# Two transposes moved behind a half product, and finer warming matmuls, in a conditional mix followed by a 6-bit linear layer

## The chip, the core and the metric

The kernel runs on one core of a Trainium2 chip. The metric is the time of one execution on the device in microseconds (us), the median of several runs. The engines are named as in the profile: PE is the matrix engine, PEld its weight loads, DVE the vector engine, ACT the scalar engine, POOL the GpSimd engine, SP the engine that issues most of the DMAs. An instruction that loads the stationary operand of a matmul is called a weight load here, whatever the operand holds.

## What is computed

The input x has 64 samples of 64 channels by 1024 columns. Each sample picks one of 16 matrices (64 by 64) and mixes its channels with it. The result goes through a linear layer whose 1024 by 1024 weights are 6-bit integers, packed four to three words of int32, with a scale and a zero point for each output column; x is added at the end:

```python
W = weights[condition]                                  # (64, 64, 64)
y = einsum('bct,bcd->bdt', x, W)
w = (unpacked.astype(float32) - zero_point) * scale     # 6 bits per weight
out = x + einsum('bsk,nk->bsn', y, w) + bias
```

All inputs and outputs are float32.

## The kernel before, in words

Two samples are one tile of 128 rows, so there are 32 tiles, in groups of four (`RING = 4`). The first group is written out by hand; a loop `Fori(1, TRIPS)` runs over the seven others. Every engine has its own program, the order of the instructions in it is the order in the text, and engines wait for each other by semaphores alone; no planner reorders anything.

For a tile PE does a `mix` (matmuls of 64 by 64, which give the mixed tile with k on the partitions, in PSUM). ACT takes its upper part (`high`, `y_hi`), DVE the rest (`low`, `y_lo`), and `products` multiplies both with the integer weights `qT`, for the left 512 or the right 512 output columns: 8 values of kt times the two parts, so 16 matmuls of 512 columns for one half of one tile. DVE scales the result (`scale_out`) and adds x, bias and the term of the zero points (`add_residual`); SP stores it.

The weights are prepared in the first group only. DVE unpacks a block of 128 output columns (`unpack_q(n)`, n from 0 to 7), PE transposes it by eight matmuls against an identity (`transpose_q(n)`, L269 to L276, into one of two PSUM banks in turn), and ACT turns it into floats and puts it into `qT` (`place_q(n)`, L440). The left half of the outputs needs blocks 0 to 3, the right half 4 to 7. `transpose_q(n)` waits for the three parts of `unpack_q(n)` and for `place_q(n - 2)`, which empties its bank. `sum_x(j)` (L411) is an ACT pass that sums the rows of tile j's input for the term of the zero points; PE's `sum_y` waits for all four of them.

Ahead of all this PE multiplies a block of zeros (`keep_warm`, L346) nine times while the first block of weights is loaded and unpacked, and twice more behind `transpose_q(0)`. Around the change PE's program reads (L375 to L395): blocks 4 and 5; the first half of tile 1's left product; block 6; the second half; block 7; the mixes of tiles 2 and 3; the sums; then the first right half, which needs all eight blocks. ACT's program reads there (L461 to L467): place blocks 4 and 5, sum tile 2, place block 6, sum tile 3, place block 7, `high` of tile 2.

Of the kernel before, what the change touches and what calls it, by code (L numbers as in the profile page):

```python
# [22 lines left out]
I16 = mybir.dt.int16  # L23

P = 128
WARMUP = 9
QCENTER = 32.0
QMASK = 63
QBITS = 6
# [3 lines left out]
def adaln_ffn(nc: bass.Bass, x, cond, weights, qweight, scale, zero, bias, out):  # L33
    B, C, K = x.shape
    NCOND, _, S = weights.shape
    N, KP = qweight.shape
    assert C == S == P // 2 and N == K
    G = KP // 3
    KT = K // P
# [11 lines left out]
    with ExitStack() as ctx:  # L51
        def sb(name, shape, dt):
            return ctx.enter_context(nc.sbuf_tensor(name, shape, dt))
# [4 lines left out]
        def sem(name):  # L58
            return ctx.enter_context(nc.semaphore(name))
# [16 lines left out]
        warm = sb("warm", [P, 512], BF16)  # L76
# [7 lines left out]
        def y_bank(slot, half):  # L84
            return y_ps[:, slot, half, :, :].rearrange("p t r -> p (t r)")
# [5 lines left out]
        free_banks = [y_bank(2, half) for half in range(2)]  # L91
# [43 lines left out]
        o_ps_ready = [sem(f"o_ps_ready{h}") for h in range(H)]  # L135
# [6 lines left out]
        def x_arrived(eng, j, i):  # L142

            eng.wait_ge(x_loaded[j % RING], (i + j // RING + 1) * 16)


        def load_q(eng, n):
            eng.dma_start(q_raw[:, n, :], qweight[n * P:(n + 1) * P, :]).then_inc(q_loaded[n], 16)
# [4 lines left out]
        def load_w_half(eng, slot, half, entry):  # L153
            rows = slice(half * S, (half + 1) * S)
            eng.dma_start(w_sb[rows, slot, :],
                          weights[bass.ds(entry, 1), :, :].rearrange("a c s -> (a c) s")
                          ).then_inc(w_loaded[slot], 16)

        def pick(eng, at):
            return eng.value_load(ids[0:1, bass.ds(at, 1)], min_val=0, max_val=NCOND - 1)  # L160

        @block.sync
        def _(sp):
# [27 lines left out]
            def store_last():  # L191
                t = TILES - 1
                store(t % RING, t // RING, 0)
                for n, (_, col, width) in enumerate(last_pieces):
                    sp.wait_ge(o_ready[1], t + 1 + n)
                    sp.dma_start(out_rows[t * P:(t + 1) * P, col:col + width],
                                 o_sb[:, t % RING, col:col + width]).then_inc(o_stored[1][t % RING], 16)
# [45 lines left out]
        def _(pe):  # L243
            def wait_mix(j, i):

                t = i * RING + j
                x_arrived(pe, j, i)
                pe.wait_ge(w_loaded[j % RING], (i + j // RING + 1) * 32)
                if not isinstance(t, int) or t >= 2:
                    pe.wait_ge(y_lo_ready, (t - 1) * 2)  # L250
# [18 lines left out]
            def transpose_q(n):  # L269
                pe.wait_ge(q_part, 3 * (n + 1))  # L270
                if n >= 2:
                    pe.wait_ge(qt_ready, n - 1)
                for kt in range(KT):
                    last = nc.tensor.transpose(qt_banks[n % 2][:, kt, :], q_cols[:, n % 4, kt * P:(kt + 1) * P],  # L274
                                               ident[:])
                last.then_inc(qt_ps_ready, 1)  # L276
# [12 lines left out]
            def products(bank, col, width, slot, kts=range(KT), parts=(y_hi, y_lo)):  # L289
                for kt in kts:  # L290
                    for part in parts:
                        last = nc.tensor.matmul(bank, part[:, slot, kt, :], qT[:, kt, col:col + width],  # L292
                                                start=(kt == 0 and part is y_hi),
                                                stop=(kt == KT - 1 and part is y_lo))
                return last
# [47 lines left out]
                last.then_inc(o_ps_ready[1], 1)  # L343


            def keep_warm(times):  # L346
                for _ in range(times):
                    nc.tensor.matmul(free_banks[1], warm[:, 0:P], warm[:], start=True, stop=True)

            def left_half(kts):  # L350
                return products(o_ps[:, 0, :], 0, NH, 1, kts)
# [2 lines left out]
                return products(o_ps[:, 0, 0:2 * P], 0, 2 * P, 0, parts=(part,))  # L354

            pe.wait_ge(warm_ready, 1)
            keep_warm(WARMUP)
            pe.wait_ge(ident_ready, 1)
            transpose_q(0)
            keep_warm(2)  # L360
            wait_mix(0, 0)
            mix(0, y_banks[0])
            transpose_q(1)
# [12 lines left out]
            transpose_q(5)  # L376
            pe.wait_ge(left_copied, 1)
            pe.wait_ge(y_lo_ready, 4)
            left_half(range(0, KT // 2))
            transpose_q(6)  # L380
            left_half(range(KT // 2, KT)).then_inc(o_ps_ready[0], 1)
            transpose_q(7)
            for j in (2, 3):
                wait_mix(j, 0)
# [24 lines left out]
        @block.scalar  # L409
        def _(act):  # L410
            def sum_x(j, i):  # L411
                x_arrived(act, j, i)
                if not isinstance(i, int) or i * RING + j >= RING:
                    act.wait_ge(ysum_ps_ready, (i * RING + j - RING + 1) * 2)
                if not isinstance(i, int) or i * RING + j >= 2:
                    act.wait_ge(xsum_ready, i * RING + j - 1)
                nc.scalar.activation(junk[:, j % 2, :], x_sb[:, j % RING, :], ACT.Copy,  # L417
                                     accum_out=xsum[:, j % RING:j % RING + 1]).then_inc(xsum_ready, 1)

            def high(j, i, banks, halves=range(2)):  # L420
                t = i * RING + j
                for half in halves:

                    act.wait_ge(y_ps_ready, t * 2 + half + 1)
                    cols = slice(half * S, (half + 1) * S)
                    nc.scalar.activation(y_hi[:, j % RING, :, cols], banks[half],  # L426
                                         ACT.Copy).then_inc(y_hi_ready, 1)

            def copy_sums(half, banks, i):

                rows = slice(half * C, (half + 1) * C)
                act.wait_ge(ysum_ps_ready, (i + 1) * 2 * RING)
                for odd in range(2):
                    place = (half + odd) % 2
                    last = nc.scalar.activation(ysum[rows, odd:RING:2],
                                                banks[half][place * S:(place + 1) * S, odd:RING:2],
                                                ACT.Copy, scale=-1.0)
                last.then_inc(ysum_ready[half], 1)

            def place_q(n):  # L440
                act.wait_ge(qt_ps_ready, n + 1)
                nc.scalar.activation(qT[:, :, n * P:(n + 1) * P], qt_banks[n % 2].bitcast(I16), ACT.Copy,  # L442
                                     bias=-QCENTER).then_inc(qt_ready, 1)

            for n in range(2):
                load_q(act, n)
            act.wait_ge(warm_ready, 1)
            nc.scalar.activation(junk[:, 1, 0:1], warm[:, 0:1], ACT.Copy)
            act.wait_ge(ids_loaded, 16)
            load_w_half(act, 0, 1, pick(act, 1))  # L450
            for n in (2, 3, 5, 7):
                load_q(act, n)
            place_q(0)
            high(0, 0, y_banks[0], range(1))
            place_q(1)
            place_q(2)
            sum_x(0, 0)
            place_q(3)
            high(1, 0, y_banks[1])
            sum_x(1, 0)  # L460
            place_q(4)  # L461
            place_q(5)
            sum_x(2, 0)
            place_q(6)
            sum_x(3, 0)
            place_q(7)
            high(2, 0, y_banks[0])  # L467
            for half in range(2):
                copy_sums(half, free_banks, 0)
            high(3, 0, y_banks[1])  # L470
            for j in range(RING):
                sum_x(j + RING, 0)

            def step(i, sums=True):
                for j in range(RING - 1):
                    high(j, i, y_banks[j])
                act.wait_ge(resid_ready, i * RING)
                for half in range(2):
                    copy_sums(half, sum_banks, i)
                high(RING - 1, i, y_banks[RING - 1])  # L480
                if sums:
                    for j in range(RING):
                        sum_x(j + RING, i)

            with act.Fori(1, TRIPS - 1) as i:
                step(i)
            step(TRIPS - 1, sums=False)
# [187 lines left out]
```

## Time and profile before

| | us |
|---|---|
| median of 3 runs | 286.48 |
| lowest, highest | 285.56, 287.77 |
| the profiled execution, whole | 285.53 |
| its span, from the first to the last instruction | 283.7 |
| PE busy | 276.5 (97% of the span) |
| DVE busy | 191.6 (68%) |
| POOL busy | 99.1 (35%) |
| ACT busy | 83.8 (30%) |

The page's clock is 1.00 in every slice. The first group takes about 40 us of the span, the loop the rest. The difference of 1.8 us between the profiled execution and its span lies around the first and the last instruction. Times within the trace are counted from the first instruction.

### The profile page before, as it was taken

How to read it: one execution, taken by the hardware profiler on the slowest of the kernel's cores; microseconds unless marked ns; L12 is line 12 of the kernel's file. 1: busy time of each engine (PE TensorE's matmuls, PEld its weight loads, DVE VectorE, ACT ScalarE, POOL GpSimd, SP SyncE). 2: the span in 40 equal slices, each digit the busy share in tenths (PEclk: the TensorE clock that was granted, in tenths of full speed). 3: DMA queues.
4: the chain of work that ended last, by engine and by line, in shares of the span. 5: the costliest groups of instructions: out<-in, count | busy, mean ns of one | idle time of the engine just before them, and what ended most of it. 6: DMA issues, size and time to landing. Idle time of an engine off the chain costs nothing.

```text
span 283.7 us, 8499 instructions
## 1 busy us (share of the span) xinstructions
PE 276.5 (97%) x3307; PEld 231.1 (81%) x3307; DVE 191.6 (68%) x261; ACT 83.8 (30%) x169; POOL 99.1 (35%) x41
## 2 busy tenths in 40 slices
PE   6999999999999999999999999999999999999995
PEld 2888887788888887988888888888888888888885
DVE  2898897785566556865559555676667655595554
ACT  3795334232044300633017310443106330060000
POOL 4005903964430444314442444404443044430000
PEclk9999999999999999999999999999999999999999
DMA  7930563456115541355114551144413552101112
GB/s 274 375 120 13 178 230 124 152 158 232 75 74 157 163 178 70 114 158 194 74 74 124 165 210 74 74 155 157 157 68 109 165 203 96 74 37 74 74 74 75
DMA packets 20278, 37.96 MB, mean 134 GB/s; under 512 B 6814, under 2 KB 7070, under 8 KB 20266
## 3 DMA queue, kind: packets, MB, share of 16 engines
q1 hardware_dynamic: 19322, 35.43, 36.4%
q10 hardware_dynamic: 944, 2.38, 2.2%
q8 instruction: 7, 0.11, 0.2%
q14 instruction: 5, 0.04, 0.1%
HBM read 21.02 MB, written 16.78 MB: 133 GB/s over the span
## 4 chain that ended last, share of the span: by engine, by line
PE 95%; DMA 2%; issue 1%; ACT 1%; DVE 0%; SPq 0%
PE o_ps L292 71%; PE y_ps L292 12%; PE y_ps L261 10%; DMA w_sb<-in_L_cond_weights_dram 1%; PE o_ps L261 1%; PE o_ps L274 0%; DMA ids<-in_itok_B_dram 0%; PE o_ps L303 0%; ACT qT L442 0%; PE y_ps L274 0%; SPq L160 0%; PE y_ps L303 0%; ACT y_hi L426 0%; DVE o_sb L621 0%; DVE o_sb L623 0%
## 5 line engine op out<-in xcount | busy, mean ns | idle before, releaser
L292 PE MATMUL o_ps<-qT,y_hi 128*128 128x512 f32 (+1 forms) x448 | 171.5, 386 | 0.6 <-ACT qT L442 0.6
L292 PE MATMUL o_ps<-qT,y_lo 128*128 128x512 f32 (+1 forms) x448 | 171.2, 385 | 0.0
L643 POOL TENSOR_TENSOR resid<-x_sb,bias_bc 128x1024 f32<-128x1024 f32 x32 | 95.8, 3000 | 151.0 <-DVE o_sb L545 130.8
L292 PEld LDWEIGHTS o_ps<-qT,y_hi 128*128 128x128 f32 x448 | 83.6, 188 | 17.5 <-ACT qT L442 0.7
L292 PEld LDWEIGHTS o_ps<-qT,y_lo 128*128 128x128 f32 x448 | 83.7, 188 | 16.8
L537 DVE TENSOR_TENSOR o_sb<-o_ps,scale_bc 128x512 f32<-128x512 f32 x54 | 37.3, 690 | 73.6 <-PE o_ps L292 73.6
L426 ACT ACTIVATE y_hi<-y_ps 128x512 fp32r<-128x512 f32 x56 | 29.4, 611 | 96.6 <-PE y_ps L261 96.2
L545 DVE TENSOR_TENSOR o_sb<-o_sb,resid 128x512 f32<-128x512 f32 x63 | 51.5, 822 | 1.9
L417 ACT ACTIVATE junk<-x_sb 128x1024 bf16<-128x1024 f32 x32 | 33.9, 1058 | 63.8 <-DMA x_sb<-in_x_dram 63.8
L526 DVE SCALAR_TENSOR_TENSOR resid<-zs_bc,ysum,resid 128x1024 f32<-128x1024 f32 x32 | 44.8, 1402 | 0.0
L516 DVE TENSOR_TENSOR y_lo<-y_ps,y_hi 128x512 fp32r<-128x512 f32 x57 | 35.6, 683 | 5.4 <-ACT y_hi L426 5.4
L261 PEld LDWEIGHTS y_ps<-w_sb,x_sb 64*64 64x64 f32 x1824 | 30.9, 135 | 3.9 <-issue 2.5
L261 PE MATMUL y_ps<-w_sb,x_sb 64*64 64x64 f32 x1824 | 32.4, 219 | 0.7 <-DMA w_sb<-in_L_cond_weights_dram 0.7
L292 PE MATMUL y_ps<-qT,y_hi 128*128 128x512 f32 (+1 forms) x80 | 29.8, 380 | 0.0
L292 PE MATMUL y_ps<-qT,y_lo 128*128 128x512 f32 (+1 forms) x80 | 28.9, 369 | 0.0
L292 PEld LDWEIGHTS y_ps<-qT,y_hi 128*128 128x128 f32 x80 | 15.1, 188 | 2.6 <-ACT qT L442 0.2
L292 PEld LDWEIGHTS y_ps<-qT,y_lo 128*128 128x128 f32 x80 | 15.1, 189 | 2.3
L261 PE MATMUL o_ps<-w_sb,x_sb 64*64 64x64 f32 x224 | 8.0, 219 | 1.2 <-issue 1.2
L261 PEld LDWEIGHTS o_ps<-w_sb,x_sb 64*64 64x64 f32 x224 | 7.2, 134 | 1.3 <-issue 1.3
L499 DVE TENSOR_SCALAR q_int<-q_raw 128x256 int16<-128x256 int16 x8 | 3.7, 460 | 4.8 <-DMA q_raw<-in_L_ffn_qweight_dram 4.8
L417 ACT ACTIVATION_READ_ACCUMULATOR junk<-x_sb 128x1 f32 x32 | 6.1, 189 | 0.0
L537 DVE TENSOR_TENSOR o_sb<-y_ps,scale_bc 128x512 f32<-128x512 f32 x8 | 5.5, 682 | 0.9 <-PE y_ps L292 0.9
(44 smaller groups left out, 69.2 us busy)
## 6 DMA issues: line engine op xcount, KB each, us to landing
x_sb<-in_x_dram SPq DMA_DIRECT2D x32, 512.0 KB, 3.4
out_dram<-o_sb SPq DMA_DIRECT2D x63, 256.0 KB, 2.1
q_raw<-in_L_ffn_qweight_dram ACTq DMA_DIRECT2D x6, 384.0 KB, 5.4
w_sb<-in_L_cond_weights_dram SPq DMA_DIRECT2D x63, 16.0 KB, 2.0
q_raw<-in_L_ffn_qweight_dram SPq DMA_DIRECT2D x2, 384.0 KB, 6.4
out_dram<-o_sb SPq DMA_DIRECT2D x2, 128.0 KB, 1.9
ids<-in_itok_B_dram SPq DMA_DIRECT2D x1, 0.2 KB
w_sb<-in_L_cond_weights_dram ACTq DMA_DIRECT2D x1, 16.0 KB, 3.4
```

The costliest lines, as they stand in the source:

```text
L261: last = nc.tensor.matmul(banks[half][part * Q:(part + 1) * Q, kt, :], x_sb[rows, slot, k0:k0 + Q], w_sb[rows, slot, :], start=True, stop= ...
L292: last = nc.tensor.matmul(bank, part[:, slot, kt, :], qT[:, kt, col:col + width], start=(kt == 0 and part is y_hi), stop=(kt == KT - 1 and ...
L417: nc.scalar.activation(junk[:, j % 2, :], x_sb[:, j % RING, :], ACT.Copy, accum_out=xsum[:, j % RING:j % RING + 1]).then_inc(xsum_ready, 1)
L426: nc.scalar.activation(y_hi[:, j % RING, :, cols], banks[half], ACT.Copy).then_inc(y_hi_ready, 1)
L499: nc.vector.tensor_scalar(to[:, :, 0], words[:, :, 0, 0], QMASK, None, ALU.bitwise_and).then_inc(q_part, 1)
L516: nc.vector.tensor_tensor(y_lo[:, j % RING, :, cols], banks[half], y_hi[:, j % RING, :, cols].bitcast(F32), ALU.subtract).then_inc(y_lo_re ...
L526: nc.vector.scalar_tensor_tensor(resid[:, j % RING, :], zs_bc[:], ysum[:, j % RING:j % RING + 1], resid[:, j % RING, :], ALU.mult, ALU.add ...
L537: nc.vector.tensor_tensor(o_sb[:, j, cols], o_banks[h] if bank is None else bank, scale_bc[:, cols], ALU.mult).then_inc(scaled[h], 1)
L545: nc.vector.tensor_tensor(o_sb[:, j, cols], o_sb[:, j, cols], resid[:, j % RING, cols], ALU.add).then_inc(o_ready[h], 1)
L643: nc.gpsimd.tensor_tensor(resid[:, j % RING, :], x_sb[:, j % RING, :], bias_bc[:], ALU.add).then_inc(xbias_ready, 1)
```

## The change

The warming matmuls ahead of the first transpose become 25 of 192 columns, in place of 9 of 512; the two behind it keep 512 columns. In PE's program `transpose_q(6)` moves from the middle of tile 1's left half to behind it, so that blocks 6 and 7 stand together. In ACT's program `sum_x(3, 0)` moves ahead of `place_q(6)`. DVE, POOL and SP have the program that they had.

```diff
-WARMUP = 9
+WARMUP = 25
+WARM_COLS = 192
...
-            def keep_warm(times):
+            def keep_warm(times, cols):
                 for _ in range(times):
-                    nc.tensor.matmul(free_banks[1], warm[:, 0:P], warm[:], start=True, stop=True)
+                    nc.tensor.matmul(free_banks[1][:, 0:cols], warm[:, 0:P], warm[:, 0:cols], start=True, stop=True)
...
-            keep_warm(WARMUP)
+            keep_warm(WARMUP, WARM_COLS)
             pe.wait_ge(ident_ready, 1)
             transpose_q(0)
-            keep_warm(2)
+            keep_warm(2, 4 * P)
...
-            left_half(range(0, KT // 2))
+            left_half(range(KT)).then_inc(o_ps_ready[0], 1)
             transpose_q(6)
-            left_half(range(KT // 2, KT)).then_inc(o_ps_ready[0], 1)
             transpose_q(7)
...
             sum_x(2, 0)
+            sum_x(3, 0)
             place_q(6)
-            sum_x(3, 0)
             place_q(7)
```

PE before, from the middle of tile 1's left half to tile 2's mix (`ident,q_int` is a transpose of a block of weights, `qT,y_hi` and `qT,y_lo` are products, `w_sb,x_sb` is a mix):

```order
L292 MATMUL o_ps<-qT,y_lo 128x512
L274 MATMUL y_ps<-ident,q_int 128x128 [waits qt_ready,q_part]
L274 MATMUL y_ps<-ident,q_int 128x128 x7
L292 MATMUL o_ps<-qT,y_hi 128x512
...
L292 MATMUL o_ps<-qT,y_lo 128x512
L274 MATMUL o_ps<-ident,q_int 128x128 [waits qt_ready,q_part]
L274 MATMUL o_ps<-ident,q_int 128x128 x7
L261 MATMUL y_ps<-w_sb,x_sb 64x64 [waits y_lo_ready,w_loaded2,x_loaded2]
```

PE with the change, the same place (line numbers are one higher):

```order
L293 MATMUL o_ps<-qT,y_hi 128x512
L293 MATMUL o_ps<-qT,y_lo 128x512
L275 MATMUL y_ps<-ident,q_int 128x128 [waits qt_ready,q_part]
L275 MATMUL y_ps<-ident,q_int 128x128 x7
L275 MATMUL o_ps<-ident,q_int 128x128 [waits qt_ready,q_part]
L275 MATMUL o_ps<-ident,q_int 128x128 x7
L262 MATMUL y_ps<-w_sb,x_sb 64x64 [waits y_lo_ready,w_loaded2,x_loaded2]
```

Before, block 6 (into `y_ps`) had eight matmuls of the left half on either side; now all sixteen stand ahead of it, and block 7 (into `o_ps`) follows at once.

ACT before, from placing block 5 to the sums (`junk,xsum` is `sum_x`):

```order
L442 ACTIVATE qT<-o_ps 128x8x128 [waits qt_ps_ready]
L417 ACTIVATE junk,xsum<-x_sb 128x1024 [waits xsum_ready,x_loaded2]
L442 ACTIVATE qT<-y_ps 128x8x128 [waits qt_ps_ready]
L417 ACTIVATE junk,xsum<-x_sb 128x1024 [waits xsum_ready,x_loaded3]
L442 ACTIVATE qT<-o_ps 128x8x128 [waits qt_ps_ready]
L426 ACTIVATE y_hi<-y_ps 128x8x64 [waits y_ps_ready] x2
```

ACT with the change:

```order
L442 ACTIVATE qT<-o_ps 128x8x128 [waits qt_ps_ready]
L417 ACTIVATE junk,xsum<-x_sb 128x1024 [waits xsum_ready,x_loaded2]
L417 ACTIVATE junk,xsum<-x_sb 128x1024 [waits xsum_ready,x_loaded3]
L442 ACTIVATE qT<-y_ps 128x8x128 [waits qt_ps_ready]
L442 ACTIVATE qT<-o_ps 128x8x128 [waits qt_ps_ready]
L426 ACTIVATE y_hi<-y_ps 128x8x64 [waits y_ps_ready] x2
```

The pass over tile 3's input now stands ahead of both placements, which follow each other directly.

## Rows read from the trace of the kernel before

**Rows 1.** The page: the span's chain of waits, by engine.

```profile
PE 95%; DMA 2%; issue 1%; ACT 1%; DVE 0%; SPq 0%
```

**Rows 2.** Timeline, 1 to 7 us: start, duration, engine, line, operation, count [idle before].

```profile
1.17 3.73 PE L348 MATMUL y_ps<-warm 128*128 128x512 bf16 x9 [1.17 <-DVE warm L552]
1.57 0.15 PEld L348 LDWEIGHTS y_ps<-warm 128*128 128x128 bf16 x1 [0.28 <-issue]
2.00 0.15 PEld L348 LDWEIGHTS y_ps<-warm 128*128 128x128 bf16 x1 [0.27 <-issue]
4.13 0.15 PEld L348 LDWEIGHTS y_ps<-warm 128*128 128x128 bf16 x1 [0.28 <-issue]
4.53 0.45 DVE L503 TENSOR_SCALAR q_int<-q_raw 128x512 int16<-128x512 int16 x1
5.12 0.61 PE L274 MATMUL y_ps<-ident,q_int 128*128 128x128 bf16 x8 [0.21 <-DVE q_int L503]
5.56 0.59 PE L348 MATMUL y_ps<-warm 128*128 128x512 bf16 x2
5.76 1.02 ACT L442 ACTIVATE qT<-y_ps 128x1024 fp32r<-128x1024 int16 x1 [2.63 <-PE y_ps L274]
6.90 1.16 PE L261 MATMUL y_ps<-w_sb,x_sb 64*64 64x64 f32 x64 [0.75 <-DMA w_sb<-in_L_cond_weights_dram]
```

**Rows 3.** Timeline of PE and its loads, 8 to 12 us: two transposes and the first products.

```profile
8.53 0.45 PEld L274 LDWEIGHTS y_ps<-ident,q_int 128*128 128x128 bf16 x8
8.54 0.62 PE L274 MATMUL y_ps<-ident,q_int 128*128 128x128 bf16 x8
9.73 1.21 PE L292 MATMUL o_ps<-qT,y_hi 128*128 128x256 f32 x8 [0.57 <-ACT qT L442]
```

**Rows 4.** Timeline of PE, 15 to 24 us, single matmuls of the left half between.

```profile
15.56 0.62 PE L274 MATMUL y_ps<-ident,q_int 128*128 128x128 bf16 x8
16.02 0.61 PE L274 MATMUL o_ps<-ident,q_int 128*128 128x128 bf16 x8
16.44 0.47 PE L292 MATMUL o_ps<-qT,y_hi 128*128 128x512 f32 x1
16.75 0.39 PE L292 MATMUL o_ps<-qT,y_lo 128*128 128x512 f32 x1
18.14 0.39 PE L292 MATMUL o_ps<-qT,y_lo 128*128 128x512 f32 x1
18.37 0.62 PE L274 MATMUL y_ps<-ident,q_int 128*128 128x128 bf16 x8
18.80 0.47 PE L292 MATMUL o_ps<-qT,y_hi 128*128 128x512 f32 x1
19.11 0.39 PE L292 MATMUL o_ps<-qT,y_lo 128*128 128x512 f32 x1
20.73 0.62 PE L274 MATMUL o_ps<-ident,q_int 128*128 128x128 bf16 x8
21.28 2.10 PE L261 MATMUL y_ps<-w_sb,x_sb 64*64 64x64 f32 x128
23.49 0.50 PE L292 MATMUL o_ps<-qT,y_hi 128*128 128x512 f32 x1
```

**Rows 5.** Timeline of ACT, 17 to 25 us.

```profile
17.14 1.02 ACT L442 ACTIVATE qT<-o_ps 128x1024 fp32r<-128x1024 int16 x1
18.99 0.20 ACT L417 ACTIVATION_READ_ACCUMULATOR junk<-x_sb 128x1 f32 x1
19.09 1.03 ACT L442 ACTIVATE qT<-y_ps 128x1024 fp32r<-128x1024 int16 x1
21.39 1.02 ACT L442 ACTIVATE qT<-o_ps 128x1024 fp32r<-128x1024 int16 x1 [0.24 <-PE o_ps L274]
22.50 1.08 ACT L426 ACTIVATE y_hi<-y_ps 128x512 fp32r<-128x512 f32 x2
23.81 0.71 ACT L435 ACTIVATE ysum<-y_ps 64x2 f32<-64x2 f32 x4 [0.23 <-PE y_ps L303]
```

**Rows 6.** Stretches: busy time of PE, PEld, DVE, ACT, POOL, clock, DMA share, GB/s.

```profile
18.00:20.00 2.00, 2.00 (x16) 1.56 (x15) 2.00 (x5) 2.00 (x5) 0.00 (x0) 1.00 0.04 8
46.00:51.00 5.00, 3.80 (x254) 3.66 (x244) 4.65 (x8) 3.04 (x6) 3.59 (x2) 1.00 0.03 7
```

**Rows 7.** Timeline of DVE, 22 to 27 us.

```profile
22.37 0.67 DVE L537 TENSOR_TENSOR o_sb<-o_ps,scale_bc 128x512 f32<-128x512 f32 x1
24.18 2.48 DVE L516 TENSOR_TENSOR y_lo<-y_ps,y_hi 128x512 fp32r<-128x512 f32 x4
```

**Rows 8.** The chain in order of time, and instruction loads by DMA, 46 to 50 us.

```profile
49.10 1.20 issue
...
q8 instruction: 1, 0.02, 1.9%
```

## Prediction

> **What bounds the kernel.** I read the chain of waits first: PE carries 95% of it, DMA 2%, and the rest is small [rows 1]. PE is busy for 276.5 of 283.7 us, so a change counts only if it shortens PE's own work, fills one of PE's few gaps, or opens a new one. The change touches two places of the first group. The timeline of the start shows the first: nine warming matmuls from 1.17 us on, the transpose of block 0 from 5.12, two more warming matmuls, and then PE idle for 0.75 us until the DMA of the first mixing matrix lands at 6.9 [rows 2]. The timeline of PE from 15 to 24 us shows the second: there every matmul starts when the one ahead of it lets it, so this stretch lies on the path without slack [rows 4]. In the loop nothing changes.
>
> **The clock at the start.** The page gives 1.00 throughout, but the spacing of the rows tells more: the warming weight loads stand 0.43 us apart (1.57, 2.00, and so on to 4.13), one for each 512 columns, which is 1.2 GHz. The ninth matmul starts at 1.17 + 8 x 0.427 = 4.58 and ends at 4.90, and two matmuls of 512 columns at 5.56 together take 0.59 us [rows 2], so by then the higher level, 2.4 GHz, is there. What PE did before the rise was 3.4 us of warming matmuls without a gap.
>
> **Part 1, the warming matmuls.** 25 x 192 = 4800 columns stand in place of 9 x 512 = 4608. At 0.427 us for 512 columns, one of 192 columns takes 0.160 us. That needs its weight load hidden: a load takes 0.15 us here [rows 2], just under 0.160; and eight transposes, whose loads and matmuls are both 128 wide, start within 0.45 us, 0.057 each, with their loads beside them [rows 3], so loads do hide behind matmuls even shorter than these. If the clock rises after the same 3.4 us of work, 21 matmuls run at the low level (21 x 0.160 = 3.36) and 4 at half of that (0.32): the last one ends at about 4.85 plus its drain, where the ninth ended before. If the rise comes late, all 25 take 4.00 us and end at 5.17, against 1.17 + 3.84 = 5.01. Block 0 is unpacked at 4.53 + 0.45 = 4.98 and its transpose starts at 5.12 [rows 2], so the delay is between 0 and 0.1 us, and even 0.1 us is taken up by the 0.75 us in which PE waits for the mixing matrix. ACT's placement of block 0 (5.76 to 6.78) is followed by a `high` that waits for this same mix. This part is worth 0. Its cover is that wait for the DMA; without it the cost would be the 0.1 us.
>
> **Part 2, block 6 behind the left half.** PE executes the same 16 products and 16 transposing matmuls. Only the joints change. A product behind a transpose takes 0.31 us to the next one (16.44 to 16.75, and 18.80 to 19.11) where the others take (18.14 - 16.75) / 6 = 0.232 [rows 4]. Before there were two such joints in the left half, now there is one: -0.08 us. A transpose followed by another takes 0.46 us (15.56 to 16.02), one followed by a product 0.43 (18.37 to 18.80): +0.03. So block 6 starts at 16.44 + 0.31 + 15 x 0.232 = 20.23, block 7 at 20.69, and the mix of tile 2 at 20.69 + 0.55 = 21.24, where it was 21.28. The sum is **-0.04 us**; from both sides, -0.08 (the joint alone) and +0.03 (no joint saved).
>
> **What waits for the moved step.** Block 6's transpose waited for nothing it does not have earlier now. Its placement on ACT comes later: it ran from 19.09, 0.72 us after the transpose began at 18.37; block 7's ran from 21.39, 0.66 after 20.73 [rows 4, 5]. With the change `place_q(6)` starts at about 20.92, and `place_q(7)` behind it, one placement being 0.92 us after the other, at 21.84, and ends at 22.86. PE needs block 6 for the sums, which begin near 23.1, and block 7 for the first right half, which starts at 23.49 [rows 4]: about 0.6 us of slack is left where 1.1 us was. `high` of tile 2, which began at 22.50, moves to about 22.76 and ends at 23.84; behind it the copies of the sums began at 23.81 [rows 5], so they are late by 0.1 us at most, and their reader on PE is 16 products further, near 27.3. DVE's `low` of tile 2 does not begin until 24.18, since DVE is busy with other work until then [rows 7], and the upper part it needs is ready by 23.84. The left half is complete earlier by 0.45 us, but DVE scales it at 22.37 anyway. Cost 0.
>
> **The moved pass over tile 3.** It can begin when tile 2's pass ends, at 19.19 [rows 5], and takes 1.15 us, until about 20.3, in time for `place_q(6)` at 20.92. It needs tile 3's input. From 18 to 20 us the DMA share is 0.04 [rows 6], so that input has landed by then. Cost 0; before, ACT was doing the same work between the two placements.
>
> **Sum.** Against the profiled execution, 285.53 + 0 - 0.04 = 285.5 us. That execution stands 0.95 us below the median of the runs, 286.48, which range over 2.2 us. A change of nothing should be expected near the median of many runs, not near a low one; I forecast **286.2 us**, between the two.
>
> **Rival A: the clock.** The moved transposes make a longer stretch without wide products: from 20.23 to about 23.45, 3.2 us, instead of 20.73 to 23.49, 2.76 us [rows 4]. If the clock fell there, the following products would run at the low level, 0.427 instead of 0.232 us, until it rose again; with 3.4 us for that as at the start, about 8 products cost 0.195 each, 1.6 us: 287.8 us. The same mechanism at the start, the narrower matmuls not letting the clock rise until a stretch like the first one has passed again, would double block 0's transpose (+0.45), the two wide warming matmuls (+0.4), the first mix (+1.1) and blocks 1 and 2 (+0.9): 2.85 less the slack of 0.75, so 2.1 us, or 288.3. It decides if the granted clock depends on wide products and not on PE being occupied. Against it: in the loop from 46 to 51 us, PE did 64-column mixes only, with 1.2 us of idle time, and the clock stood at 1.00 [rows 6]. Chance 0.07. The Trainium skill speaks against this change here: its page TensorE: Matmul & The Clock Gate, Part 4, says that transposes do not count as busy time for the clock. No row here shows the clock falling behind a transpose; by that page the cost would be that of this rival.
>
> **Rival B: instruction loading.** In the first pass of the loop PE stops for 1.20 us at 49.10 for nothing but "issue", in the middle of the fourth mix, and an instruction load by DMA falls into that stretch [rows 8]. The mixes use instructions fastest, 64 matmuls with their loads in 1.1 us. The change puts 16 more matmuls and 16 loads ahead of everything, so what is loaded when shifts by 32 instructions. If the stretch with the shortage now falls across another piece of work, the stop could vanish (-1.2, 285.0) or a second one appear where blocks 6 and 7 and two mixes follow each other (+1.2, 287.4). I expect the stop to stay, some 0.3 us earlier in the same mix: 32 instructions are a sixteenth of the four mixes' 512. Chance 0.07, either way.
>
> **Rival C: the loads are not hidden (slower).** Its place is the warming row alone. If a weight load and a 192-column matmul ran one behind the other at the low level, a pair would take 0.15 + 0.16 = 0.31 us, 25 of them 7.75 us, to 8.92 instead of 4.90: the first mix would start behind the transpose and the two wide ones at about 10.5 instead of 6.9, +3.6 us, 289.8. If the clock rises on time only 11 are that slow and the end is near 6.6, +0.5 us. It decides from 0.23 us a pair on, where 4.0 + 1.75 us eats up the 0.75 of slack. Against it stands the transposes' spacing of 0.057 us with equal loads [rows 3]. Chance 0.02.
>
> **Rival D: the change gains more.** The first transpose could start sooner if fine matmuls leave less to finish; but it waits for DVE (until 4.98), and the mix for a DMA. Worth 0.1 at most, and hidden. A gain over 1% has no mechanism that I can find; I leave it 0.02 for what I have not seen.
>
> **Numbers.** My forecast has 0.82. What can be told from no change is 1%, 2.9 us. Its own uncertainty is that of medians drawn from runs that range from 285.5 to 287.8. Those and rival B give a range from 285.1 to 287.6, which leaves out most of A and C. Slower by over 1% (above 289.3) needs C whole or both halves of A, or one half with an unlucky draw: 0.05. Faster by over 1%: 0.02. Within 1%: 0.93.
>
> **What would show it.** Right: 25 warming matmuls from 1.17 to between 4.8 and 5.2, the mix at 6.9; block 6 at 20.23, block 7 at 20.69, the mix of tile 2 at 21.24; placements at 20.92 and 21.84; the right half at about 23.45; one stop of 1.2 us near 49. Wrong: PE idle with ACT as its releaser before the sums or the right half, products spaced by more than 0.3 us anywhere, the first mix later than 7, or a second stop in the first group's mixes.

## The result

The changed kernel takes 286.93 us in the median of 22 runs (285.76 to 287.87), the kernel before 285.88 (285.41 to 287.77). The ratio is 1.0027, with a 95% interval from 1.0014 to 1.0040. The forecast was 286.2 us. The time lies in the range that was forecast, and 1 us is far below 1%, but it is clear of noise, and the forecast's sum had a gain of 0.04 us. Some mechanism of about 1 us was missing from it.

The profile of the changed kernel is of an execution of 287.39 us with a span of 285.6, against 285.53 and 283.7. PE's timeline from 6.8 to 25.4 us, which answers to [rows 2, 4]:

```profile
6.84 1.16 PE L262 MATMUL y_ps<-w_sb,x_sb 64*64 64x64 f32 x64
...
8.99 0.62 PE L275 MATMUL y_ps<-ident,q_int 128*128 128x128 bf16 x8 [0.43 <-DVE q_int L503]
...
12.54 0.62 PE L275 MATMUL o_ps<-ident,q_int 128*128 128x128 bf16 x8 [0.55 <-DVE q_int L503]
14.29 1.16 PE L262 MATMUL y_ps<-w_sb,x_sb 64*64 64x64 f32 x64 [1.13 <-DMA w_sb<-in_L_cond_weights_dram]
...
18.37 0.47 PE L293 MATMUL o_ps<-qT,y_hi 128*128 128x512 f32 x1
...
22.11 0.62 PE L275 MATMUL y_ps<-ident,q_int 128*128 128x128 bf16 x8
22.57 0.61 PE L275 MATMUL o_ps<-ident,q_int 128*128 128x128 bf16 x8
23.11 2.10 PE L262 MATMUL y_ps<-w_sb,x_sb 64*64 64x64 f32 x128
...
25.31 0.50 PE L293 MATMUL o_ps<-qT,y_hi 128*128 128x512 f32 x1
```

The piece that was rearranged went as forecast, even a little better: from the start of the left half to the mix of tile 2 it takes 23.11 - 18.37 = 4.74 us where it took 21.28 - 16.44 = 4.84 [rows 4]. But it starts 1.93 us later. Nothing was lost up to the mix of tile 0, at 6.84 (6.90 before [rows 2]); all of it is lost between there and the mix of tile 1, in three waits for loads: for blocks 2 and 3 of the weights (PE waits there for DVE, which unpacks them and itself waits for their DMAs), and for tile 1's matrix. Part of this is a draw of this execution (the matrix was issued 0.45 us late, as it is in some executions of any of these kernels). A second profile of the same kernel (`e0_after_again` below) has the issue on time and the same loss. Its waits from 8 to 16 us:

```profile
PE y_ps L262 <- DMA w_sb<-in_L_cond_weights_dram: 1.5, 1, 1.5
PE y_ps L275 <- DVE q_int L503: 0.6, 1, 0.6
```

Tile 1's matrix comes in two DMAs. Their time from issue to landing, for the kernel before:

```profile
L155 SPq DMA_DIRECT2D w_sb<-in_L_cond_weights_dram x2: 470/474/477, 5.7 to 6.3; - x2
...
DMA to landing us min/median/max: 5.7/5.7/5.7
```

and for the second profile of the changed one:

```profile
L156 SPq DMA_DIRECT2D w_sb<-in_L_cond_weights_dram x2: 478/520/562, 5.7 to 6.3; - x2
...
DMA to landing us min/median/max: 5.7/6.6/7.5
```

One half lands as fast as ever, the other 1.8 us later. What else used the DMA engines then? The queues from 10 to 12.4 us, the kernel before (packets, MB, share of 16 engines):

```profile
q1 hardware_dynamic: 325, 0.63, 69.9%
q10 hardware_dynamic: 121, 0.31, 34.3%
```

and the second profile of the changed kernel:

```profile
q1 hardware_dynamic: 294, 0.54, 60.1%
q10 hardware_dynamic: 145, 0.38, 40.7%
q8 instruction: 1, 0.02, 2.8%
```

The third row is new: a packet of 16 KB of instructions. A share of 2.8% of 16 engines over 2.4 us is 0.028 x 16 x 2.4 = 1.1 us on one engine, which could be the larger part of the late half's 1.8 us. In the kernel before the first such load comes later, at 12.9 us, when tile 1's matrix has landed.

### The profile page after: what moved, and what is told of

The parts are those of the page before. It is cut to its first block, busy times and chain, and to the rows that moved or that the text cites. A ratio compares the mean times of both kernels' runs of the same rounds, so it can differ in the third digit from the quotient of the medians.

```text
span 285.6 us, 8531 instructions
## 1 busy us (share of the span) xinstructions
PE 277.8 (97%) x3323; PEld 234.1 (82%) x3323; DVE 192.6 (67%) x261; ACT 83.7 (29%) x169; POOL 99.2 (35%) x41
## 4 chain that ended last, share of the span: by engine, by line
PE 93%; DMA 3%; SPq 1%; issue 1%; DVE 0%
PE o_ps L293 69%; PE y_ps L293 12%; PE y_ps L262 10%; DMA w_sb<-in_L_cond_weights_dram 3%; PE o_ps L262 1%; DMA ids<-in_itok_B_dram 1%; SPq L161 1%; SPq L156 0%; PE o_ps L304 0%; PE y_ps L275 0%; PE o_ps L275 0%; SPq L167 0%; PE y_ps L304 0%; DVE o_sb L621 0%; DVE o_sb L623 0%
## 5 line engine op out<-in xcount | busy, mean ns | idle before, releaser
L526 DVE SCALAR_TENSOR_TENSOR resid<-zs_bc,ysum,resid 128x1024 f32<-128x1024 f32 x32 | 45.7, 1431 | 0.0
L349 PE MATMUL y_ps<-warm 128*128 128x192 bf16 (+1 forms) x27 | 5.1, 381 | 1.2 <-DVE warm L552 1.2
```

What stands on the lines that cost most here:

```text
L349: nc.tensor.matmul(free_banks[1][:, 0:cols], warm[:, 0:P], warm[:, 0:cols], start=True, stop=True)
L526: nc.vector.scalar_tensor_tensor(resid[:, j % RING, :], zs_bc[:], ysum[:, j % RING:j % RING + 1], resid[:, j % RING, :], ALU.mult, ALU.add ...
```

## The experiments

All were run beside the kernel before on their own chip; each ratio is to that kernel there, whose median was 285.76 to 286.09 us. A pair is a warming matmul with its weight load.

### The change taken apart

The changed kernel again (`e0_after_again`): no edit.

> The changed kernel once more, beside the three below, as the yardstick. All theories: the ratio to the kernel before is near 1.0027 (interval 1.0014 to 1.0040 so far), 0.3 to 1.2 us slower. If the first mix of tile 1 waits again for its matrix (1.13 us in the first profile) and blocks 2 and 3 come late, the loss lies in the loads; if these waits are gone and the time is still longer, it lies elsewhere.

287.04 us, ratio 1.0047 (1.0020 to 1.0075). The loss is in the loads, as shown above.

`e1_warm_only` is the diff without the moved lines:

```diff
-WARMUP = 9
+WARMUP = 25
+WARM_COLS = 192
```

> The kernel before with 25 warming matmuls of 192 columns in place of 9 of 512; blocks 6 and 7 where they were. Theory W (the loss comes with the warming matmuls: by their number, their 32 more instructions, or the clock that rises later): ratio 1.002 to 1.004, nearly all of the loss. Theory M (the loss comes with the moved blocks: less slack for ACT or DVE): ratio 1.000. Theory D (the change does nothing, and the profiled run is one of the slow draws that the kernel before has as well, up to 287.8 us): ratio 1.000.

286.80 us, ratio 1.0024 (1.0003 to 1.0046). Its mix of tile 1 waits 1.1 us for the matrix, one half of which lands 6.9 us after its issue. So far theory W. But the other part of the diff alone (`e2_move_only`) is no cheaper:

```diff
-            left_half(range(0, KT // 2))
+            left_half(range(KT)).then_inc(o_ps_ready[0], 1)
             transpose_q(6)
-            left_half(range(KT // 2, KT)).then_inc(o_ps_ready[0], 1)
             transpose_q(7)
...
+            sum_x(3, 0)
             place_q(6)
-            sum_x(3, 0)
```

> The kernel before with blocks 6 and 7 behind the left half and the pass over tile 3 ahead of both placements; 9 warming matmuls of 512 columns. Theory W: ratio 0.9995 to 1.000 (my sum of -0.04 us, and the two traces show -0.10 us between the start of the left half and the mix of tile 2). Theory M: ratio 1.002 to 1.004. Theory D: 1.000.

286.70 us, ratio 1.0040 (1.0019 to 1.0061). Each part alone costs about what both together cost; neither theory W nor M foresaw that. The chain of waits of this kernel from 20 to 25 us shows a loss of another kind:

```profile
20.61 0.46 PE y_ps L275 x8
21.07 0.45 PE o_ps L275 x8
21.52 1.55 PE y_ps L262 x94
23.07 0.52 issue
23.59 0.69 PE y_ps L262 x31
```

In the middle of the mixes of tiles 2 and 3, PE stops for "issue", as it did once at 49.10 in the kernel before [rows 8]. I read both as PE being out of instructions; that is inferred from the instruction load that falls beside each stop (here at 21.09 us). From the mix of tile 2 (21.45) to the first mix of the loop (46.47) it takes 25.02 us, where it took 24.21 (21.28 to 45.49): 0.8 us, the loss of the medians. The changed kernel has no such stop there (the two mixes above start at 23.11 and the products follow at 25.31, 2.20 us, against 2.21 before).

`e3_count_only` adds 16 matmuls of one column to the kernel before:

```diff
+            keep_warm(16, 1)
             keep_warm(WARMUP, WARM_COLS)
```

> The kernel before with 16 further warming matmuls of a single column ahead of the 9 of 512: as many instructions on PE as the changed kernel has (16 matmuls and 16 loads more), hardly more time. If the loss comes from the shift of the instruction stream by 32 (instructions are loaded by DMA while the weights are, the first 16 KB load at about 10.5 us rather than 12.9): ratio 1.002 to 1.004. If it comes from the narrow matmuls themselves or from the clock: 1.000, at most +0.1 us hidden behind the wait for the first matrix.

286.82 us, ratio 1.0034 (1.0019 to 1.0049). The 16 pairs, with the 9 wide matmuls kept, cost all of it. They are nearly but not quite free in PE's time: in this profile the warming lasts 4.45 us in place of 3.73, the clock rises late, and the first mix begins at 7.26, 0.36 us later than before. About a third of the loss can be that; the rest lies elsewhere.

### Is the comparison fair, and is it the columns?

`e5_before_copy` is the kernel before, with no edit.

> The kernel before, unchanged, run as if it were a changed one. All three changed versions so far came out 0.9 to 1.1 us slower, the warming alone and the move alone each as much as both together, so the comparison itself has to be tested. If it is fair: ratio 1.000, interval within 0.998 to 1.002. If whatever is not the reference series reads 1 us longer: ratio 1.003.

285.91 us, ratio 1.0006 (0.9980 to 1.0031). It is fair.

`e4_cols_only`:

```diff
-WARMUP = 9
+WARMUP = 10
+WARM_COLS = 480
```

> The kernel before with 10 warming matmuls of 480 columns: the same 4800 columns as the changed kernel, but only 2 more instructions on PE. Theory I (the shift of PE's instruction stream by 32 makes its first 16 KB load fall at about 11 us, among the loads of weights, and one half of tile 1's matrix lands 1.1 to 1.8 us later; seen in all three profiles with 25 narrow matmuls, 11.4, 11.2 and 10.8 us, and not in the three others, 12.9 to 13.0 us): ratio 1.000, the instruction load near 12.9 us, no wait of the mix of tile 1. Theory C (columns or time spent at the low clock): 1.002 to 1.004.

285.66 us, ratio 0.9991 (0.9962 to 1.0021). The columns cost nothing. (The profiled execution took 286.71, more than the median, and does not show the waits of the median.)

The move and the count without narrow matmuls (`e6_move_and_count`):

```diff
+            keep_warm(16, 1)
             keep_warm(WARMUP, WARM_COLS)
...
             transpose_q(6)
             transpose_q(7)
```

> The blocks moved as in the change, and 16 warming matmuls of one column ahead of the 9 of 512. Theory I and its second half (with the move alone, the instructions for the mixes of tiles 2 and 3 come too late, a stop of 0.5 us that the shift by 32 takes away): the stop in these mixes is gone, and the time is that of the count alone or the changed kernel, 286.8 to 287.0, ratio 1.003 to 1.004. If instead the two losses are of another kind and add up: 287.7, ratio 1.006.

287.08 us, ratio 1.0034 (1.0011 to 1.0057): the changed kernel's time, no stop in the mixes of tiles 2 and 3, and the two losses do not add up. Tile 1's matrix is on time here (5.8 us for both halves), so it is not what all these kernels lose by. Blocks 4 and 6 are late: they land 7.5 and 8.0 us after their issue (6.0 and 6.8 before). DVE unpacks block 4 ahead of `low` of tile 1, and the left half needs that `low`. DVE and then PE:

```profile
14.39 0.48 DVE L500 TENSOR_SCALAR q_int<-q_raw 128x256 int16<-128x256 int16 x1 [1.79 <-DMA q_raw<-in_L_ffn_qweight_dram]
...
16.25 1.27 DVE L517 TENSOR_TENSOR y_lo<-y_ps,y_hi 128x512 fp32r<-128x512 f32 x2
...
17.67 0.47 PE L293 MATMUL o_ps<-qT,y_hi 128*128 128x512 f32 x1 [0.66 <-DVE y_lo L517]
```

In the kernel before:

```profile
12.90 0.47 DVE L499 TENSOR_SCALAR q_int<-q_raw 128x256 int16<-128x256 int16 x1 [0.47 <-DMA q_raw<-in_L_ffn_qweight_dram]
```

This wait of DVE for block 4 is 1.8 to 2.3 us in the profiles of the changed kernel (both), `e1`, `e6` and `e11`, so a late block delays the left half whether the matrix is late or not.

### The dose

> The kernel before with 13 warming matmuls of 354 columns, no blocks moved. Theory I: first instruction load at 12.9 us, ratio 1.000. If any rise in the number of warming matmuls costs time in proportion (1.0 us for 16 more): 4 more cost 0.25 us, ratio 1.001.

> The kernel before with 64 warming matmuls of 72 columns (4608 columns), 110 more instructions. Theory I: the first instruction load comes in the mix of tile 0, at 8 to 9 us, with the load of weights at its full 400 GB/s; other loads are held up by it, 286.5 to 287.5, ratio 1.002 to 1.006, and the second load falls between 14 and 16 us. If only a load at 11 us does harm, because of what is on its way then: 1.000. At 72 columns a weight load (0.15 us at the low clock) is longer than its matmul (0.06), so the warming may take up to 64 x 0.11 = 7 us and cost 2 us more by itself; the first transpose's start tells.

> The whole change, but with 13 warming matmuls of 354 columns (4602 columns) in place of 25 of 192, so 8 more instructions on PE than before, not 32. Theory I: 8 instructions leave PE's first instruction load at 12.9 us, behind the loads of weights, so tile 1's matrix and blocks 4 and 6 land on time (5.8 and at most 6.8 us after their issue, not 6.9 to 8.1); and they bring the second load, at 21.1 us with the move alone, 0.9 us forward (8 instructions are 4 products of 0.23 us), to about 20.2, so that the stop of 0.5 us in the mixes of tiles 2 and 3 is gone. Time 285.7 to 286.0, ratio 0.999 to 1.001. If the moved blocks themselves cost the time (less slack for ACT and DVE): 286.7 or more, ratio 1.003 to 1.004, as with the move alone.

> The kernel before with 17 warming matmuls of 271 columns, 16 more instructions, no blocks moved. Theory I: ratio 1.000 with the first instruction load at 12.9 us, 1.003 with it at 11, the same as with the moved blocks. Cost in proportion to the number: 1.0015.

> The whole change with 17 warming matmuls of 271 columns (4607), 16 more instructions on PE than before. Theory I, both halves: the second instruction load comes at about 19.6 us (21.1 with 0 and 20.5 with 8 instructions more), the stop in the mixes of tiles 2 and 3 is gone or under 0.1 us, and if the first load stays at 12.9 us the loads of weights land on time: 285.7 us, ratio 0.998 to 1.000, the best version. If 16 instructions already bring the first load forward to 11 us: 286.8 with the signature of the changed kernel. If the moved blocks cost in themselves: 286.7 with no late load and no stop.

> The same with 21 warming matmuls of 220 columns (4620), 24 more instructions. No stop in the mixes of tiles 2 and 3. Theory I: the time follows the first instruction load, 285.7 us with it at 12.9 us, 286.9 with it at 11; I expect the latter, since 24 is near the changed kernel's 32. The moved blocks costing in themselves: 286.7 either way.

> The kernel before with 21 warming matmuls of 220 columns, no blocks moved: 12 additional pairs. Theory I with the step between 12 and 16 pairs, as the moved kernel with 21 had it: 285.8, ratio 0.999 to 1.001, first instruction load at 12.8 us. In proportion: 286.5.

Each differs from the kernel before or from the changed one only in the two numbers, as 13 and 354:

```diff
-WARMUP = 25
-WARM_COLS = 192
+WARMUP = 13
+WARM_COLS = 354
```

| more pairs | blocks in place: us, ratio | blocks moved: us, ratio |
|---|---|---|
| 0 | 285.91, 1.0006 (0.9980 to 1.0031) | 286.70, 1.0040 (1.0019 to 1.0061) |
| 4 | 285.74, 0.9989 (0.9963 to 1.0015) | 286.78, 1.0038 (1.0010 to 1.0066) |
| 8 | 285.72, 0.9993 (0.9976 to 1.0011) | 286.72, 1.0017 (0.9996 to 1.0039) |
| 12 | 285.69, 0.9997 (0.9965 to 1.0030) | 285.88, 0.9999 (0.9980 to 1.0018) |
| 16, narrow | 286.80, 1.0024 (1.0003 to 1.0046) | 287.04, 1.0047 (1.0020 to 1.0075) |
| 16, of one column | 286.82, 1.0034 (1.0019 to 1.0049) | 287.08, 1.0034 (1.0011 to 1.0057) |
| 55 | 286.86, 1.0031 (1.0014 to 1.0048) | |

This is not a slope but two steps. Down the first column the time stands at 285.7 to 285.9 up to 12 pairs and at 286.8 from 16 on, and 55 cost no more than 16. In the second there is one step more, in the other direction: with 0 and 4 pairs the moved blocks cost 0.7 to 0.9 us, with 12 nothing, and from 16 on the first step is there again. With 8 pairs the median is 0.8 us higher, but the interval of the ratio reaches 0.9996, so this one is not clear of noise by itself. I had expected the stop in the mixes gone at 4 and at 8 pairs, from a spacing of 0.23 us a product; that was wrong. The profile with 4 pairs (an execution of 285.97, faster than its median) has 0.2 us of it left, with the weights on time. The one with 8 pairs has more, in the waits of PE over the span:

```profile
PE o_ps L262 <- issue: 1.0, 1, 1.0
PE y_ps L262 <- issue: 0.9, 1, 0.9
```

and the one with 12 has only the stop in the loop (its second row is the wait ahead of the first warming matmul):

```profile
PE o_ps L262 <- issue: 1.6, 1, 1.6
PE y_ps L349 <- DVE warm L552: 1.2, 1, 1.2
```

When the instruction load comes fits this. The queues with 8 pairs, from 20.9 to 22 us:

```profile
q8 instruction: 1, 0.02, 5.2%
```

With 12 pairs, from 19 to 20.9 us:

```profile
q8 instruction: 1, 0.02, 3.5%
```

Neither kernel has such a row in the other's stretch. The mix of tile 2 starts at 20.97 and 21.01 in these two, and goes through 64 pairs of instructions a tile in 1.1 us. The size of the stop roughly follows how long ahead of this mix the load begins: 0.06 us behind its start with 8 pairs (0.9 us of stop), 0.4 us ahead with 0 and with 4 (0.5 and 0.2), and 1.5 us or more ahead with 12, in the kernel before and in the changed one (none). For the other step: the row of instruction loads between 10.5 and 12.4 us is there in five of the seven profiles with 16 pairs or more and all the weights (the changed kernel twice, `e1`, `e6`, `e11`), and blocks 4 and 6 land 7.1 to 8.1 us after their issue in all five. It is absent in all profiles of 0 to 12 pairs. It is not the only thing that makes these blocks late: with 8 pairs in place, in an execution of 287.29 us, they were issued up to 0.9 us late and landed after 6.9 and 7.5 us, with the load at 13.5 us; `e4` is similar. The other two profiles with 16 pairs are of the kernel with the count alone.

> A second look at the kernel with 16 further warming matmuls of one column. Its median was 286.8, but the profiled execution was its fastest, 285.87, with the first instruction load at 12.9 us. Theory I: an execution of 286.5 to 287.2 shows that load at about 11 us and blocks 4 and 6 landing more than 7 us after issue; one near 285.9 shows 12.9 us again.

This execution took 286.20 us, between the two levels, with its instruction load at 12.47 us, not from 10.5 to 12.4, and blocks 4 and 6 landing after 6.1 and 7.5 us. Neither of this kernel's two profiles (285.87 and 286.20, both faster than its median of 286.82) shows an instruction load at 11 us. So 16 pairs do not fix the time of that load; what its slower executions look like is not shown.

### Is it the collision?

The load of instructions was so far only seen together with the late weights. Two kernels with 1.18 MB less to load, without and with the 16 further matmuls of one column, take the crowd away. They leave out the loads of blocks 5, 6 and 7 and unpack block 4 in their place, so the outputs of these columns are wrong:

```diff
-            for n in (4, 6):
+            for n in (4,):
...
-            for n in (2, 3, 5, 7):
+            for n in (2, 3):
...
-                dve.wait_ge(q_loaded[n], 16)
-                words = q_raw[:, n, :].bitcast(I16).rearrange("p (g w e) -> p g w e", w=3, e=2)
+                m = min(n, 4)
+                dve.wait_ge(q_loaded[m], 16)
+                words = q_raw[:, m, :].bitcast(I16).rearrange("p (g w e) -> p g w e", w=3, e=2)
```

> The kernel before with blocks 5, 6 and 7 of the weights not loaded; block 4's words are unpacked in their place (the outputs of these columns are those of block 4's weights). It is the base of the next one: 1.15 MB less, about 2.9 us of the 400 GB/s stretch, so that the DMA engines are no longer full from about 10 us on. At or below the kernel before, ratio 0.996 to 1.000.

> The same, blocks 5, 6 and 7 not loaded, with 16 further warming matmuls of one column. Theory I (instruction load and weight loads collide): within 0.3 us of the one without them, against 1.0 us where all blocks are loaded. If the shift costs for another reason (PE's own stream, the clock that rises later, the warming that ends 0.3 us later): 0.9 to 1.1 us slower than the one without.

The base measured 286.03 us (ratio 1.0008, 0.9972 to 1.0043) and 285.91 with the further pairs (0.9991, 0.9965 to 1.0017). The 16 pairs that cost 0.9 us when all weights are loaded show no cost here; the interval against the kernel before leaves room for 0.5 us at most. The matrix of tile 1 lands after 4.0 and 4.2 us at most. So most of the 0.9 us is neither PE's own time nor the clock: it needs the crowd of loads. That the instructions' packet is what delays them is the reading that fits, and is not shown by itself. The profiled execution of the base has its instruction load at 11.3 us, without any pair added, and no late block; but it took 287.60 us, far above its median. With the pairs the load came at 12.45 us. So the number of instructions is not all that sets the time of a load, and no profile here has the load at 11 us with 16 pairs and the light traffic.

## Why the prediction was wrong

**The step that failed** is in part 1: "This part is worth 0. Its cover is that wait for the DMA". For PE's time this holds: the mix of tile 0 starts at 6.84 with the change and at 6.90 without. In the count-alone kernel it held less well, with 0.36 us at the first mix. But the term was not 0: the warming alone costs 0.9 us in the median (286.80, `e1`). The 16 more pairs are also 32 instructions to be loaded. The price was paid not where the matmuls run but from 11 us on, by blocks of weights that land 0.7 to 1.7 us later and, in four of five profiles, by tile 1's matrix, in the same profiles in which the first instruction load starts at 10.8 to 11.5 us in place of 12.9. I had the instruction stream as rival B, and gave it 0.07, but asked only when PE stops for it (which stayed a single stop, as I expected: 1.1 us in the first profile, 1.6 in the second, 1.2 before, and 1.6 for the unchanged kernel run again). I never asked what the load itself may push aside, though the DMA engines moved 391 GB/s from 10 to 12.4 us. That the 32 instructions cost this and that it takes the crowded loads is shown by the count alone and by the few loads; the step between, one packet delaying the others, stays inferred.

**The moved blocks, -0.04 us,** were measured at -0.10 for the stretch itself, and the terms around them held: no wait for ACT before the sums or the right half, in either profile of the changed kernel. But the sum of this part failed as well, since it left out PE's instructions. Alone, the move costs 0.8 to 0.9 us (286.70). The reading that fits is that the instruction load begins only 0.4 us ahead of 128 fast pairs, where it began 1.5 us ahead; it is a stop that I named in rival B with the wrong cause, the further instructions. With 12 of them it is gone. So with the 16 pairs the changed kernel pays for late weights, and is spared the stop.

**The base** was right in kind, since the profiled execution was near the lowest of 285.4 to 287.8, but 286.2 was 0.3 us high: the median of the kernel before was 286.48 over 3 runs and is 285.88 over 22. By that luck the forecast missed by 0.7 us, though its mechanism missed by 1.1.

**Rival A, the clock,** did not happen in the stretch of moved transposes: products after it are 0.23 us apart. The Trainium skill, TensorE: Matmul & The Clock Gate, Part 4, says that transposes do not count as busy for the clock; no row here shows an effect of that. At the start the clock rises later in some executions, whichever warming is used. The changed kernel's first transposes took 1.06 us; so did those of the kernel before when run again:

```profile
5.12 1.01 PE L274 MATMUL y_ps<-ident,q_int 128*128 128x128 bf16 x8
5.93 1.00 PE L348 MATMUL y_ps<-warm 128*128 128x512 bf16 x2
6.86 1.16 PE L261 MATMUL y_ps<-w_sb,x_sb 64*64 64x64 f32 x64
```

Eight transposes in 1.01 us and two wide matmuls in 1.00 are near the 1.2 GHz level, against 0.61 and 0.59 in [rows 2], and the mix starts at the same time: the 0.75 us of slack covers it.

**Rival C** fell: 25 narrow matmuls end 4.18 us after they begin with the clock low, and in 3.73 with the clock rising on time, the duration of the nine; their loads are hidden. Its threshold of 0.23 us a pair was too high: the warming may last from 1.17 to about 5.87 (the transpose at 5.12 plus the 0.75 of slack), which is 0.19 a pair; 0.15 to 0.17 was measured.

**What stays open:** which of the transfers share an engine with the instructions' packet, and whether it is what delays them; what besides the number of instructions sets the time of a load, since 55 pairs bring it to the same 11 us as 16, and not to 9 as I expected, and 8 pairs with the moved blocks leave the second load at 21.0 us where none had it at 21.1. No version beats the kernel before: 12 further pairs with the moved blocks come out level with it, 0.9999 (0.9980 to 1.0018).

## What to carry to other kernels

Instructions are data that are loaded too: on an engine that runs through many short ones, an edit that adds or reorders them can move the loads of those behind it. Here such edits cost 0.8 to 1.1 us, once where the engine stopped beside a load and once where a load fell among transfers that were waited for. So ask of a "free" instruction not only who waits behind it but also what its loading meets. Measure it by a control that adds instructions and hardly anything else, and try several doses: a step points to timing and not to work.

## What the runs showed of the hardware

- PE's instructions come in packets of 16 KB, seven in this kernel, each of which takes 0.9 to 1.7 us. With one of them among loads at 390 GB/s, half of a 32 KB matrix landed 1.1 to 1.8 us later in four of five profiles, and blocks of 384 KB up to 1.7 us later in all five. The Trainium skill, Runtime: NRT & Kernel Launch, section Instruction fetch mechanics, has blocks of 256 instructions, loaded ahead by the engine's own queue, and calls the cost of a crossing mostly hidden. The size of the packets and the queue of their own agree with the rows here. Most of the seven are hidden too; the exceptions are the one or two that fall beside a stretch of 64-wide matmuls (0.2 to 1.7 us a stop) and, as inferred, the one that falls among awaited transfers (0.9 us in the median).
- The level of TensorE's clock in the first 7 us differs between executions of one and the same kernel: behind the same nine warming matmuls, the eight transposes took 0.61 us in one and 1.01 us in another.
